# An audio-tower kernel in which four low-part products of the first FFN product become two pairs on row halves

## What is computed

```python
h = _L0_tok_ref(x, ...)                                  # 128 tokens of 192 features
h = h + _L0_attn_ref(_layernorm(h, axis=-1), Wq, Wk, Wv, Wo)
xt = _layernorm(h, axis=-1)
g = gelu(einsum('td,hd->th', xt, in_weight) + in_bias)   # in_weight (768, 192)
h = h + einsum('th,ho->to', g, out_weight)
```

## Time and profile before

| | before |
|---|---|
| median of 3 executions | 1053.89 us |
| profiled execution, its span | 1053.71 us, 1051.8 us |
| PE busy, PEld busy | 998.5 us (95%), 866.3 us (82%) |
| DVE, ACT, POOL busy | 814.6 us (77%), 733.9 us (70%), 435.2 us (41%) |
| DMA | 127.49 MB, mean 121 GB/s |

### The profile page before, as it was taken

One profiled execution on the slowest core, in us unless ns is written; L12 is line 12 of the kernel. 1 busy time (PEld: TensorE's weight loads), 2 busy tenths in 40 slices (PEclk: granted clock), 3 DMA queues, 4 the chain that ended last, 5 costly groups with the idle time before them and its releaser, 6 DMA issues. The chain is left out here.

```text
span 1051.8 us, 24498 instructions
## 1 busy us (share of the span) xinstructions
PE 998.5 (95%) x7232; PEld 866.3 (82%) x7232; DVE 814.6 (77%) x2095; ACT 733.9 (70%) x2530; POOL 435.2 (41%) x583
## 2 busy tenths in 40 slices
PE   3689999999999999999999999999999999999987
PEld 2577888888988888888888888888889888888865
DVE  2678888778878877888877888887788787788861
ACT  2456777777776677677777777677867777777761
POOL 0334444443544343454444444434345444434440
PEclk7789999999999999999999999999999999999999
DMA  5134434334434434443433454343444344334331
GB/s 174 43 106 134 133 107 143 117 110 127 147 118 116 138 109 118 136 142 110 130 124 106 125 147 126 108 142 112 118 130 146 116 119 132 111 113 146 115 112 45
DMA packets 139935, 127.49 MB, mean 121 GB/s; under 512 B 30992, under 2 KB 123024, under 8 KB 139920
## 3 DMA queue, kind: packets, MB, share of 16 engines
q1 hardware_dynamic: 137632, 124.16, 39.5%
q10 hardware_dynamic: 2288, 3.15, 0.9%
HBM read 70.63 MB, written 56.62 MB: 121 GB/s over the span
## 5 line engine op out<-in xcount | busy, mean ns | idle before, releaser
L403 POOL TENSOR_TENSOR E<-E,e_rcp 128x512 f32<-128x512 f32 x192 | 198.7, 1042 | 284.7 <-DVE e_rcp L534 281.6
L302 ACT ACTIVATE E<-ring,m_neg 128x128 f32<-128x128 f32 x768 | 272.0, 389 | 56.3 <-DVE m_neg L514 56.3
L395 POOL TENSOR_TENSOR q_tok<-rot_c,rot_s 128x384 f32<-128x384 f32 x128 | 125.8, 1005 | 132.7 <-DVE rot_s L492 132.7
L302 ACT ACTIVATION_READ_ACCUMULATOR E<-ring,m_neg 128x1 f32 x768 | 174.7, 227 | 0.0
L514 DVE TENSOR_REDUCE m_neg<-ring 128x4 f32<-128x512 f32 x192 | 122.7, 681 | 57.0 <-PE ring L710 57.0
L296 ACT COPY qkT<-ring 128x512 f32<-128x512 f32 x128 | 71.9, 588 | 128.3 <-PE ring L689 128.3
L525 DVE STREAM_TRANSPOSE EB<-E 128x512 f32<-128x512 f32 x192 | 134.3, 699 | 17.7 <-POOL E L403 17.7
L834 PE MATMUL ring<-wo_sb,OT 128*128 128x192 f32 x768 | 139.6, 332 | 1.5 <-ACT OT L310 1.5
L697 PE MATMUL bank<-wout_sb,G 128*128 128x192 f32 x768 | 135.4, 326 | 2.8 <-ACT G L369 2.8
L697 PEld LDWEIGHTS bank<-wout_sb,G 128*128 128x128 f32 x768 | 125.4, 190 | 3.4 <-ACT G L369 3.3
L834 PEld LDWEIGHTS ring<-wo_sb,OT 128*128 128x128 f32 x768 | 124.1, 191 | 3.9 <-issue 2.4
(11 more groups left out here) (122 smaller groups left out, 2275.9 us busy)
## 6 DMA issues: line engine op xcount, KB each, us to landing
spill<-EB SPq DMA_DIRECT2D x64, 512.0 KB, 2.7
ET<-spill SPq DMA_DIRECT2D x256, 128.0 KB, 2.8
spill<-EB SPq DMA_DIRECT2D x64, 256.0 KB, 2.1
ET<-spill SPq DMA_DIRECT2D x256, 64.0 KB, 2.3
x_sb<-in_x_dram SPq DMA_DIRECT2D x64, 192.0 KB, 2.5
out_dram<-out_sb SPq DMA_DIRECT2D x64, 96.0 KB, 2.3
x_sb<-in_x_dram SPq DMA_DIRECT2D x64, 64.0 KB, 2.3
w_raw<-in_w_att_dram ACTq DMA_DIRECT2D x2, 576.0 KB, 4.8
```

Of the source, the lines that this page charges most:

```text
L302: last = nc.scalar.activation(E[:, a, s * P:(s + 1) * P], RING[a][:, s * P:(s + 1) * P], ACT.Exp, bias=m_neg[:, a, s:s + 1], accum_out=e_s ...
L395: nc.gpsimd.tensor_tensor(q_tok[:, a, c], rot_c[:, a, c], rot_s[:, a, c], ALU.add).then_inc(q_out, 1)
L403: nc.gpsimd.tensor_tensor(e, e, r, ALU.mult).then_inc(prob_out, 1)
```

## The change

In blocks 0 to 3 the product of the last 64 features with the low part HL is made by itself, with contraction 64, ahead of everything else of `ffn_first`. A new tile of weights F2D holds the rounded last 64 features on both halves of the partitions. Block 0 takes rows 0 to 63 of F2D and HL, block 2 rows 64 to 127, then block 1 and block 3 likewise: four products of 64 x 256, neighbours on different row halves and to different banks. The term low weight times low input, which F2S added in these four blocks, is no longer added. Blocks 4 and 5 keep their five products, with F2S and HL first. All waits except that for the scores' bank stand ahead of the first product, and the first of them is now for HL_out in place of HH_out. F2D is one more rounding copy on ScalarE when the kernel starts.

```diff
-        FH1, FL1, F2S = (sb(n, [P, HID], F32R) for n in ("FH1", "FL1", "F2S"))
+        FH1, FL1, F2S, F2D = (sb(n, [P, HID], F32R) for n in ("FH1", "FL1", "F2S", "F2D"))
...
                         nc.scalar.copy(F2S[:], win_raw[:, HID:2 * HID]).then_inc(s_hi, 1)
+                        nc.scalar.copy(F2D[:], win_raw[:, HID:2 * HID]).then_inc(s_dup, 1)
...
                 def ffn_first():
-                    pe.wait_ge(HH_out, p)
-                    for j, bank in enumerate(HIDDEN):
-                        if j == 0:
-                            need(pe, res_out, p - 1)
-                        if j == 1 and tok:
-                            pe.wait_ge(h_out, n + 1)
-                        if j == 2 and att:
+                    h1h, h2h = (HH[:, k].rearrange("p a t -> p (a t)") for k in range(2))
+                    h1l, h2l = (HL[:, k].rearrange("p a t -> p (a t)") for k in range(2))
+
+                    def columns(m):
+                        return HIDDEN[m // 2][:, (m % 2) * DP:(m % 2 + 1) * DP], slice(m * P, (m + 1) * P)
+
+                    pe.wait_ge(HL_out, p)
+                    need(pe, res_out, p - 1)
+                    if tok:
+                        pe.wait_ge(h_out, n + 1)
+                    for m, rows in ((0, slice(0, D2)), (2, slice(D2, P)), (1, slice(0, D2)), (3, slice(D2, P))):
+                        dst, c = columns(m)
+                        nc.tensor.matmul(dst, F2D[rows, c], h2l[rows], start=(m % 2 == 0), stop=False)
+                    for m in range(NM):
+                        dst, c = columns(m)
+                        if m == 4 and att:
                             pe.wait_ge(exp_out, 6 * p + 3 + GROUPS.index(1) + 1)
-                        for m in (2 * j, 2 * j + 1):
-                            c = slice(m * P, (m + 1) * P)
-                            h1h, h2h = (HH[:, k].rearrange("p a t -> p (a t)") for k in range(2))
-                            h1l, h2l = (HL[:, k].rearrange("p a t -> p (a t)") for k in range(2))
-                            for i, (w, h) in enumerate(((FH1, h1h), (FL1, h1h), (F2S, h2h), (FH1, h1l), (F2S, h2l))):
-                                if m == 0 and i == 3:
-                                    pe.wait_ge(HL_out, p)
-                                last = nc.tensor.matmul(bank[:, (m % 2) * DP:(m % 2 + 1) * DP], w[:, c], h,
-                                                        start=(i == 0), stop=(i == 4))
-                        last.then_inc(hid_mm, 1)
+                        if m >= 4:
+                            nc.tensor.matmul(dst, F2S[:, c], h2l, start=(m == 4), stop=False)
+                        nc.tensor.matmul(dst, FH1[:, c], h1h, start=False, stop=False)
+                        nc.tensor.matmul(dst, FL1[:, c], h1h, start=False, stop=False)
+                        nc.tensor.matmul(dst, F2S[:, c], h2h, start=False, stop=False)
+                        last = nc.tensor.matmul(dst, FH1[:, c], h1l, start=False, stop=(m % 2 == 1))
+                        if m % 2 == 1:
+                            last.then_inc(hid_mm, 1)
```

More of the change, by code:

```diff
@@ L154, in program @@
             sem(n) for n in ("s_scaled", "s_bd", "s_hi", "s_lo", "s_zero", "s_warm"))
-        s_warm_exp, s_padded = sem("s_warm_exp"), sem("s_padded")
+        s_warm_exp, s_padded, s_dup = sem("s_warm_exp"), sem("s_padded"), sem("s_dup")
         pool_passed, dve_passed = sem("pool_passed"), sem("dve_passed")
@@ L843, in step @@
                     pe.wait_ge(s_lo, 4)
+                    pe.wait_ge(s_dup, 1)
                 if att:
```

## The result

The changed kernel takes 1043.97 us (median of 7 runs, 1042.99 to 1046.6), the kernel before 1052.04 us (median of 7). One of the seven runs before, of 3463.57 us, is a slow one and is left out of the ratio. The ratio is 0.9934, 95% interval 0.9922 to 0.9946: 1052.04 x 0.0066 = 6.9 us less, between 5.7 and 8.2; the medians themselves are 8.1 apart. The forecast was 1047.0 us and 6.7 us less. The difference was forecast well and the time itself 3.0 us too high, of which 1.7 are the profiled run of 1053.71 that the forecast started from, where the later median is 1052.04. By the 2% that was called measurable this is no change; by this comparison alone it is a small gain, and its interval excludes 1.

What follows compares the result with a forecast made beforehand. TensorE, 99% busy, was taken to bound the 31.00 us step. Thirty steps at 0.237 us less, plus 0.4 at the end, gave 6.7 us off the profiled 1053.71: 1047 us, range 1043 to 1051.

Steps and rivals of the forecast that it cites:

- The products that come: In `ffn_first`, four products of contraction 64 run as two pairs, costing 0.237 us in place of 0.474.
- The change of arrangement: Between scores and `ffn_first`, going from row halves to all rows costs about 0.2 us, paid once before and after; nothing added.
- The wait that moves: Ahead of the first pair, the wait for HL has 0.2 us left less some 0.05; counted as 0.
- What then waits: Behind the pairs, with TensorE 0.24 us earlier, all later waits hold, with 0.04 us to spare at the least.
- just in time: At `output(0)`, the first OT copy is there at 558.46 at the latest, for a start at 558.50 before.
- the tightest place: At `tok_qk`, the wait for the GELUs moves with `x_turned`, so the whole 0.24 us passes.
- The size of the step: In the steady loop, each step gains 0.237 us, and the period goes from 31.00 to 30.76 us.
- Start and end: Added copy at the start costs 0; step 31 loses its gain; step 32 costs 0.4 us more.
- held up beside: Rival, 12%: a tight place (HL, OT, XL, GELUs) takes back 0.1 to 0.2 us a step; 1049 to 1053 us.
- No pairs: Rival, 8%: float32r products on row halves go one after the other, no gain, 0.4 us added at the end; 1054 us.
- loads in the open: Rival, 3%: a half's weights can't load while it streams, so each pair costs 0.22 us; 1053 us.
- A new arrangement with every product: Rival "Slower", 3%: each float32r product on a half drains the array and pays 0.22 us; 12.7 us more, 1066 us.

Runs made afterwards that it cites:

- all_low: The changed kernel with all four separate low-part products on rows 0 to 63, so none lies beside another half; period 30.995 us.
- pairs_later: The changed kernel with the two pairs behind block 3's last product instead of behind the scores; period 31.133 us, 0.4% slower than the kernel before.
- wait_head: The kernel before with only the waits for HL and h_out moved ahead of the first product; period 30.998 us, ratio 1.001.
- the pair of runs with HL late: The kernel before and the changed kernel, each with VectorE making HL behind its first maximum of the scores; periods 31.633 and 31.951 us.
- exp11: The changed kernel with one of the second sequence's twelve exponentials left out in the loop on ScalarE; period 30.733 us.
- no_low4: The changed kernel without the four separate low-part products; period 30.733 us, ratio to the kernel before 0.9901.
- aabb: The changed kernel with the four separate products in the order block 0, 1 (rows 0 to 63), 2, 3 (rows 64 to 127); period 30.754 us.

## Why the prediction was right

- **The products that come: 0.237.** Measured on TensorE: the first full product starts 0.238 later against the scores, and the two pairs of starts are there. Two of the signs named for it were off. The first pair stands 0.04 behind the last scores and not 0.11, and the pairs stand 0.20 apart and not 0.12, close to the 0.22 that was to mean open loads. The loads, 0.11 apart, and the sum of the distances say that it isn't that; why the 0.20 is there is not shown. all_low has it too, between products of one half. The step's sentence "a pair of passes on two row halves costs what one pass on all rows does" was carried from float32 scores to float32r products, and holds. That it is the pairing that pays is shown by all_low, which lost the whole gain.
- **The change of arrangement: nothing added.** Shown from the other side by pairs_later: 0.400 for two changes. The estimate of about 0.2 each held.
- **The wait that moves: 0.** wait_head shows it (30.998). I reckoned 0.2 us of room less 0.05. Room up to the load is 0.11, less the 0.05 that the load takes to follow, since the first pair came sooner behind the scores than a full distance; and what the pair of runs with HL late shows is that there is no second cover behind it.
- **What then waits.** Here two sentences were off and cancelled, which was luck and not reckoning. `output(0)` was called "just in time": its loads were 0.07 late. The copy was over in time, 553.30 - 546.47 = 6.83 behind the scores where I had 558.46 - 551.52 = 6.94, but I compared it with the start of the product, while the load has to come ahead of the product and follows the copy's end by 0.11. `tok_qk` behind the GELUs was called "the tightest place", and it was the place that gave the 0.07 back: I had it that the wait "moves with `x_turned`" and the whole 0.24 passes, but TensorE came only 0.18 earlier and the GELUs 0.247, so the wait that had cost 0.07 there cost nothing any more. exp11 shows that it is the GELUs that set the place: there TensorE came earlier and lost it again. XL cost nothing.
- **The size of the step: 0.267 and not 0.237.** This is the mis-sized term. 0.247 of it stands between the scores of sequence 2 and the next `scores(0)`; it is 0.01 more than four products less two pairs at 0.1186. The other 0.02 lies in the second half of the step and is not explained. Over 30 steps the 0.03 a step are 0.9 us, inside the interval of the ratio.
- **Start and end: +0.4.** The added copy starts at 33.53 and takes the 0.83 forecast, and ScalarE idles for 5.06 us soon behind it (6.18 in the earlier trace rows): it cost nothing. The last step cost 0.32 at a clock of 0.96; at the clock that I had assumed, that of the earlier trace rows, the one distance more would be longer. Step 31 shows no gain, as forecast: its period is 21.786 against 21.691 and 21.873 in the two profiles of the kernel before, which is no finer a reading than 0.2 us.
- **The sum.** 30 x 0.267 - 0.32 = 7.7 us by these terms, 6.9 [5.7, 8.2] by the ratio, 6.7 forecast. The time, 1043.97, lies below the 1045 to 1048 that the forecast proper named and near the low end of 1043, which had been set for the scatter of the runs; that scatter is the clock's. Two figures of the rivals don't follow from their terms: held up beside gives 1050 to 1053 and not 1049, and to be slower by 2% a new arrangement would have to cost some 0.29 a product, 1.3 times the 0.22 and not twice.
- **The rivals.** No pairs is excluded by the rows of the changed kernel and by all_low, loads in the open by the loads and by what the four cost (0.24, not 0.44). A new arrangement with every product is excluded by the same. Held up beside was given 12%; its mechanism does exist. It stands directly behind this change and took nothing from it on balance; no_low4 ran into it at once.

## What to carry to other kernels

Products that use half of the rows pay only beside products of the other half (0.12 us a pair saved here), and a change of arrangement costs 0.2 us, more than one pair saves: put them next to work that already has the arrangement. Every pair here also wrote to two different banks; a pair to one bank was not tried. A wait that is moved forward is free only as far as something ahead of it covers it; measure the distance to the weight load, not to the product. Before the next cut on the engine that bounds, leave the work out altogether for one run: here it would have shown that nothing more was to be had until a second road got shorter too.

## What was not expected of the hardware

- TensorE ran the third product of a list beside the first and the fourth beside the second, by the records' banks (aabb, period 30.754).
- A product of 64 rows on a half that is still streaming follows after 0.12 us, its load under way 0.1 us before (all_low).
- A weight load that waits for a copy of ScalarE starts 0.11 us behind the copy's end (553.30 to 553.41, 552.88 to 552.99), one that waits for GELUs, exponentials or HL 0.05 (557.94 to 557.99). The copy's row takes 0.63 us right behind an exponential against 0.59 after a gap, but it begins 0.14 before the row ahead of it ends (552.67, 552.81).
- The granted clock over the last 15 us is 0.85 to 0.89 in some profiles and 0.95 to 0.99 in others, and over the first 85 us 0.80 to 0.84, with the same instructions too. Each end makes 1 to 2 us of the span that no instruction explains, more than the 0.4 us that the last step was worth.
